# Two token-mixing layers on one core: the first block of h turned between two halves of the B combination, the folded kernel rounded by output, and the last LoRA products put among the last output's products

## The chip, the cores and the metric

The kernel runs on one core of a Trainium2 chip, as one launch. The metric is the device time of that core in microseconds (us), lower is better. Every matrix product is made from numbers split in two parts, a rounded high part and the rest, so each product of the reference costs three matmuls (high by high, low by high, high by low).

## The reference, cut to what matters

Two layers follow each other on 64 items of 32 tokens, 512 features wide. Layer 0 multiplies each item by one of 8 matrices (chosen by the item's id), then adds a plain linear layer with a gated LoRA; layer 1 is a gated MLP with per-item adapters and then a linear layer with a LoRA whose rank each token picks.

```python
# layer 0
h = einsum('bsi,boi->bso', x, weight[adapter_ids])            # "cond": one of 8 matrices per item
base_out = h @ kernel + bias
A_eff = einsum('bn,nri->bri', gate, lora_A)                    # 8 groups, 16 LoRAs of rank 32
B_eff = einsum('bn,nor->bor', gate, lora_B)
x = x + base_out + B_eff @ (A_eff @ h) + B_shared @ (A_shared @ h)
# layer 1
g, u = x W_gate + lora, x W_up + lora                          # adapters by item
h = silu(g) * u ; h = h W_down + lora
out = h W + b
scores = h @ gate_w.T + gate_b ; probs = softmax(scores)       # 4 ranks, one is picked
x = x + out + (rank-masked) h A B
```

## The kernel before, in words

The code is written by hand, engine by engine (one function each for sync, gpsimd, scalar, vector and tensor), and the order of each engine's instructions is the order of the lines; semaphores are the only link between engines. Names ending in `_hi` and `_lo` are the two parts of a number: ScalarE (ACT) makes the high part by a rounding copy (`high`, L644), VectorE (DVE) the low part as the difference (`low`, L868). Tokens are cut in NTB = 4 blocks of TB = 512.

The stages, with the time at which they run in the profile of before:

- **Sorted blocks**, up to 84.7 us. The items are sorted by their matrix into NBLK = 22 blocks of 128 rows, and the result h goes by indirect DMA (GpSimd, L573) to a scratch area in HBM in the items' own order. ACT and DVE empty the PSUM banks in turn (`evacuate`).
- **Gated A and B.** `la` (lora_a) and `gsel` (the gates spread over a diagonal) are split while the last sorted blocks run. TensorE (PE) then makes A_eff in psG and psU (48 matmuls of 256 columns), and B_eff in two halves j = 0, 1 in banks 0 and 1 of psD (12 matmuls of 512 columns each, four blocks' worth in all). ACT copies the even block of each half to `b_eff` (L714), DVE the odd one (L1119). ACT also splits `kraw`, the plain kernel with the shared LoRA folded in, in one instruction over 2048 columns.
- **First layer**, four blocks. `turn_h0(t)` turns a block of h by 16 transposes (L1475) from `tok` in SBUF into four PSUM banks psX, psT, psG, psU; `tok` is loaded from the scratch by `load_h0` on the sync queue (L513) once all scatters have landed. `high_h0` and `low_h0` split the four banks one after another into `ht`. Then come the A products into psX (L1501, L1502), `kern(o)` for the four outputs o (12 matmuls each into psD) and `lora(o)` (L1371, L1372), and DVE adds the result into x_all.
- **Gated MLP**, four blocks of 11 hidden chunks (166 to 628 us), untouched by the change.
- **Second layer**, four blocks (631 us to the end). `linear(o)` makes output o in bank o of psD (12 matmuls). `routed(t+1)` makes the next block's rank scores in psX. `turn_scores` (the four transposes of L1663) sends the scores to DVE, which runs a chain of small instructions (softmax, the pick, L1308 to L1330) to a mask `mexp`; `turn_mask` (L1671) transposes that into psU, DVE multiplies it in (`r`, L1339), ACT and DVE split `r`, and the LoRA products of the four outputs (L1366, L1367) end the block. DVE adds each output into x_all (L1345) and the sync queue stores it (L561).

Two waits of PE stand for what the change touches:

```python
                    elif o == 0:
                        pe.wait_ge(S["beff_even"], NTB // 2)
                        pe.wait_ge(S["beff_odd"], NTB // 2)
                        pe.wait_ge(S["kern_lo"], 1)
```

Of the kernel before, what the change touches and what calls it, by code (L numbers as in the profile page):

```python
# [128 lines left out]
def two_layers(nc, a, out):  # L129
    with ExitStack() as ctx:  # L130
# [179 lines left out]
        gsel_at = wh_at + slot_bytes  # L310
# [331 lines left out]
        def _(act):  # L642
# [44 lines left out]
            for b in range(NBLK):  # L687
                if b % 2 == 0:
                    evacuate(b)
                if b + AHEAD < NBLK:  # L690
                    high_xs(b + AHEAD)
                if b % W_EVERY == 0 and b // W_EVERY + 2 < N_COND:
                    high_w(b // W_EVERY + 2)
                if b == NBLK - AHEAD:
                    act.wait_ge(S["lora_a_in"], 16)
                    multiplied(act, 16)
                    high(la_hi[:], lora_a[:], S["la_hi_s"])
            act.wait_ge(S["gsel_f"], 1)
            high(g_hi[:], gsel[:], S["g_hi_s"])
# [11 lines left out]
            high(k_hi[:], kraw[:], S["kern_hi"])  # L711
            for j in range(NTB // 2):
                act.wait_ge(S["beff_ps"], j + 1)
                act.activation(b_eff[:, 2 * j, :], psD[0:R2, j, :], ACT.Copy).then_inc(S["beff_even"], 1)  # L714
            act.wait_ge(S["beff_even"], 1)
# [4 lines left out]

            high_be(0)
# [144 lines left out]
        def _(dve):  # L866
# [220 lines left out]
            for b in range(NBLK):  # L1087
# [10 lines left out]
                if b == NBLK - AHEAD:  # L1098
                    dve.wait_ge(S["gate_in"], 16)
                    dve.tensor_tensor(gsel[:].rearrange("p k (g r) -> p (k g) r", r=RANK0),  # L1100
                                      cst("delta").unsqueeze(1).broadcast_to([P, 4 * GROUPS, RANK0]),
                                      gate_v[:].rearrange("p k g -> p (k g)").unsqueeze(2)
                                      .broadcast_to([P, 4 * GROUPS, RANK0]), ALU.mult).then_inc(S["gsel_f"], 1)
                    dve.wait_ge(S["la_hi_s"], 1)
                    low(la_lo[:], lora_a[:], la_hi[:], S["la_lo_s"])
                if b == NBLK - AHEAD + 1:
                    dve.wait_ge(S["g_hi_s"], 1)
                    low(g_lo[:], gsel[:], g_hi[:], S["g_lo_s"])
# [6 lines left out]
            dve.wait_ge(S["kern_hi"], 1)  # L1115
            low(k_lo[:], kraw[:], k_hi[:], S["kern_lo"])
            for j in range(NTB // 2):
# [8 lines left out]

            low_h0(0)

# [225 lines left out]
        def _(pe):  # L1354
# [104 lines left out]
            for j in range(NTB // 2):  # L1459
# [3 lines left out]
                mm.then_inc(S["beff_ps"], 1)  # L1463
            pe.wait_ge(S["aeff_done"], 2)
# [13 lines left out]
            turn_h0(0)  # L1478

            def first_layer(t):  # L1480
                hi, lo = HT0[t % 2]

                def kern(o):
                    if t:
                        pe.wait_ge(S["x1_f"], C * (t - 1) + o + 1)
                    elif o == 0:
                        pe.wait_ge(S["beff_even"], NTB // 2)
                        pe.wait_ge(S["beff_odd"], NTB // 2)
                        pe.wait_ge(S["kern_lo"], 1)
# [159 lines left out]
            def second_layer(t):  # L1649
                hi, lo = HT2[t % 2]  # L1650

                def linear(o):
                    if t:
                        pe.wait_ge(S["out_v"], C * (t - 1) + o + 1)
                    for c in range(C):
# [4 lines left out]
                linear(0)  # L1660
                pe.wait_ge(S["r_sb"], 2 * t + 1)
                for s in range(SUB):
                    mm = pe.transpose(psG[:, s * NR:(s + 1) * NR], scores[RMAX:RS, s * P:(s + 1) * P],  # L1663
                                      ident[RMAX:RS, RMAX:RS])
                mm.then_inc(S["sc_ps"], 1)
                linear(1)
                linear(2)
                pe.wait_ge(S["mexp_s"], NR * (t + 1))
                pe.wait_ge(S["xa_m"], 2 * t)
                for s in range(SUB):  # L1670
                    pe.transpose(psU[0:RMAX, s * P:(s + 1) * P], mexp[:, s, :], ident).then_inc(S["mask_ps"], 1)  # L1671
                linear(3).then_inc(S["lin_ps"], 1)
                if t < NTB - 1:
                    routed(t + 1)
                pe.wait_ge(S["xa_hi"], t + 1)
                pe.wait_ge(S["xa_lo"], t + 1)
                for o in range(C):
# [71 lines left out]
```

## Time and profile before

| | us |
|---|---|
| median of 3 runs | 707.62 |
| lowest, highest | 703.88, 852.61 |
| the profiled execution, device time | 704.56 |
| its span, first to last instruction | 702.3 |
| PE busy in the span | 673.9 (96%) |
| DVE, ACT, POOL busy | 313.7, 294.0, 338.9 |
| mean granted TensorE clock | 0.995 |

The device time is 2.3 us more than the span. The profile shows one core; busy time of PE is modelled, so that matmuls in a row overlap slightly in the rows and their spacing, not their duration, is what one costs.

### The profile page before, as it was taken

To read this page: it belongs to the slowest core of one execution; us is meant where nothing else is said; L and a number is where in the kernel's file an instruction comes from. 1 tells how busy PE (TensorE), PEld (TensorE's weight loads), DVE (VectorE), ACT (ScalarE), POOL (GpSimd) and SP (SyncE) were. 2 spreads that over 40 slices of the span, in tenths; PEclk is the share of its full clock that TensorE was granted. 3 is DMA by queue.
4 is the path that set the end of the run, shared out by engine and by line. 5 is a ranking of instruction groups with operands and counts; after the bars stand their busy time and mean duration, and the time that the engine had idled before them with its cause. 6 is when DMAs were issued, how large, how long until landed. Compare 5 with 4: busy or idle time off the path is not lost.

```text
span 702.3 us, 11052 instructions
## 1 busy us (share of the span) xinstructions
PE 673.9 (96%) x3340; PEld 560.6 (80%) x3340; DVE 313.7 (45%) x723; ACT 294.0 (42%) x626; POOL 338.9 (48%) x262
## 2 busy tenths in 40 slices
PE   5799989998999999999999999999999999989997
PEld 3678778887788888888888888888888888867775
DVE  3778667645512222732222462242273134234664
ACT  2775553323633332653333464343265343334210
POOL 0134400231687666388666578776638867400000
PEclk9999999998999999999999999999999999999999
DMA  8963461121354346245335245434425524200112
GB/s 315 381 252 138 179 225 61 44 70 46 97 164 134 109 137 232 82 152 161 114 115 175 58 142 167 128 112 135 153 77 159 155 92 139 86 1 1 61 67 113
DMA packets 32209, 91.79 MB, mean 131 GB/s; under 512 B 5312, under 2 KB 5440, under 8 KB 30624
## 3 DMA queue, kind: packets, MB, share of 16 engines
q1 hardware_dynamic: 21936, 61.05, 25.9%
q0 software_dynamic: 10080, 30.16, 13.1%
q8 instruction: 21, 0.34, 0.2%
q14 instruction: 28, 0.23, 0.1%
q10 hardware_dynamic: 144, 0.00, 0.0%
HBM read 81.23 MB, written 9.96 MB: 130 GB/s over the span
## 4 chain that ended last, share of the span: by engine, by line
PE 86%; DVE 5%; ACT 3%; issue 2%; DMA 2%; DVEq 1%; ACTq 0%; POOL 0%; SPq 0%
PE psD L1360 10%; PE psD L1361 9%; PE psD L1362 9%; PE psG L1360 6%; PE psG L1362 6%; PE psG L1361 6%; PE psU L1360 6%; PE psU L1362 6%; PE psU L1361 6%; PE psD L1435 2%; PE psD L1436 2%; PE psD L1437 2%; PE psG L1367 1%; PE psG L1366 1%; PE psX L1360 1%
## 5 line engine op out<-in xcount | busy, mean ns | idle before, releaser
L568 POOL TENSOR_TENSOR gu_lo<-gu_raw,gu_hi 128x1024 fp32r<-128x1024 f32 x44 | 113.0, 2568 | 104.6 <-ACT gu_hi L644 104.3
L1245 DVE TENSOR_TENSOR act_f<-psU,silu 128x512 f32<-128x512 f32 x44 | 30.4, 692 | 186.1 <-ACT silu L810 186.1
L599 POOL DMA_INDIRECT ab<-in_ab,idx_tab x88 | 85.5, 972 | 20.8 <-issue 17.4
L810 ACT ACTIVATE silu<-psG 128x512 f32<-128x512 f32 x44 | 26.2, 596 | 151.3 <-PE psG L1367 151.2
L1360 PE MATMUL psG<-x_hi,gu_hi 128*128 128x512 f32 x176 | 72.6, 413 | 1.2 <-ACT silu L810 1.2
L1360 PE MATMUL psD<-act_hi,dn_hi 128*128 128x512 f32 x176 | 69.1, 393 | 0.0
L1361 PE MATMUL psD<-act_lo,dn_hi 128*128 128x512 f32 x176 | 69.1, 392 | 0.0
L1362 PE MATMUL psG<-x_hi,gu_lo 128*128 128x512 f32 x176 | 69.0, 392 | 0.0
L1360 PE MATMUL psU<-x_hi,gu_hi 128*128 128x512 f32 x176 | 68.9, 392 | 0.0
L1361 PE MATMUL psG<-x_lo,gu_hi 128*128 128x512 f32 x176 | 68.8, 391 | 0.0
L1362 PE MATMUL psD<-act_hi,dn_lo 128*128 128x512 f32 x176 | 68.7, 390 | 0.0
L1362 PE MATMUL psU<-x_hi,gu_lo 128*128 128x512 f32 x176 | 68.6, 390 | 0.0
L1361 PE MATMUL psU<-x_lo,gu_hi 128*128 128x512 f32 x176 | 68.5, 389 | 0.0
L568 POOL TENSOR_TENSOR dn_lo<-dn_raw,dn_hi 128x512 fp32r<-128x512 f32 x44 | 57.2, 1301 | 22.6 <-ACT dn_hi L644 22.6
L573 POOL DMA_INDIRECT h_scratch<-h,idx_s x22 | 23.7, 1075 | 63.2 <-ACT h L673 31.6
L602 POOL DMA_INDIRECT ad_raw<-in_ab,idx_down x44 | 45.0, 1022 | 13.4 <-issue 13.4
L644 ACT ACTIVATE gu_hi<-gu_raw 128x1024 fp32r<-128x1024 f32 x44 | 46.2, 1051 | 11.2 <-DMA gu_raw<-in_gu 11.0
L868 DVE TENSOR_TENSOR act_lo<-act_f,act_hi 128x512 fp32r<-128x512 f32 x44 | 30.6, 696 | 30.7 <-ACT act_hi L644 30.7
L644 ACT ACTIVATE act_hi<-act_f 128x512 fp32r<-128x512 f32 x44 | 27.8, 632 | 33.3 <-DVE act_f L1245 33.3
L1360 PEld LDWEIGHTS psG<-x_hi,gu_hi 128*128 128x128 f32 x176 | 33.2, 189 | 10.7 <-issue 1.2
L868 DVE TENSOR_TENSOR ad<-psX,ad 128x128 fp32r<-128x128 f32 x44 | 12.8, 291 | 63.0 <-ACT ad L644 62.8
L1435 PE MATMUL psD<-cond_w_hi,xs_t_hi 128*128 x88 | 35.6, 404 | 4.7 <-DVE cond_w_lo L868 4.7
(324 smaller groups left out, 1594.8 us busy)
## 6 DMA issues: line engine op xcount, KB each, us to landing
gu_raw<-in_gu SPq DMA_DIRECT2D x44, 512.0 KB, 3.4
dn_raw<-in_dn SPq DMA_DIRECT2D x44, 256.0 KB, 4.3
cond_w_raw<-in_cond_w SPq DMA_DIRECT2D x8, 1024.0 KB, 6.7
x_all<-in_x_t SPq DMA_DIRECT2D x4, 1024.0 KB, 9.5
tok<-h_scratch SPq DMA_DIRECT2D x4, 1024.0 KB, 5.5
out_t<-x_all SPq DMA_DIRECT2D x16, 256.0 KB, 2.1
ab<-in_ab,idx_tab POOLq DMA_INDIRECT x88, 3.8
kraw<-in_kern SPq DMA_DIRECT2D x1, 1024.0 KB, 11.5
```

The costliest lines, as they stand in the source:

```text
L568: pool.tensor_tensor(dst, x, hi, ALU.subtract).then_inc(s, 1)
L573: pool.indirect_dma_start(h0_dram, bass.IndirectOffsetOnAxis(idx_s[:, b:b + 1], 0), h0[:, ring, :], None).then_inc(S[f"c_st{ring}"], 16)
L599: pool.indirect_dma_start(ab[:, par, g, :], None, a["ab"], bass.IndirectOffsetOnAxis(idx_tab[:, NGT * t + g, fc:fc + 1], 0)).then_inc(S[f" ...
L602: pool.indirect_dma_start(ad_raw[:, par, :], None, a_rows, bass.IndirectOffsetOnAxis(idx_down[:, t, fc:fc + 1], 0)).then_inc(S[f"ad_in{par ...
L644: act.activation(dst, x, ACT.Copy).then_inc(s, 1)
L810: act.activation(silu[:], psG[:], ACT.Silu).then_inc(S["silu_s"], 1)
L868: dve.tensor_tensor(dst, x, hi, ALU.subtract).then_inc(s, 1)
L1245: dve.tensor_tensor(act_f[:], psU[:], silu[:], ALU.mult).then_inc(S["act_f_s"], 1)
L1360: pe.matmul(ps, wh, xh, start=start, stop=False, skip_group_check=True)
L1361: pe.matmul(ps, wh, xl, start=False, stop=False, skip_group_check=True)
L1362: return pe.matmul(ps, wl, xh, start=False, stop=stop, skip_group_check=True)
L1435: pe.matmul(ps, xh, w[0], start=c == 0, stop=False)
```

## The change

It moves instructions; the arithmetic stays. In five places:

1. The gates `gsel`, with their two parts, lie in slot 3 of the matrices' area instead of slot 1. Slots 0 and 1 are where the first block's `ht` goes, slots 2 and 3 the second block's.
2. In the sorted blocks, the splitting of `lora_a` and of `gsel` is written at other block numbers.
3. PE turns the first block of h between the two halves of the B combination. ACT and DVE split it right after they have taken out the first half.
4. `kraw` is split in four instructions of 512 columns, by output o, two ahead of the first block's splitting and two behind. `kern(o)` of the first block waits for its own part only.
5. In the second layer, `turn_scores` comes before `linear(0)` for the blocks t > 0; in the last block, `turn_mask` comes before `linear(2)`, and the LoRA products of outputs 0 to 2 stand in the middle of `linear(3)`.

```diff
-        gsel_at = wh_at + slot_bytes
+        gsel_at = wh_at + 3 * slot_bytes
...
-                if b == NBLK - AHEAD:
+                if b == NBLK - 4:
                     act.wait_ge(S["lora_a_in"], 16)
                     multiplied(act, 16)
                     high(la_hi[:], lora_a[:], S["la_hi_s"])
-            act.wait_ge(S["gsel_f"], 1)
-            high(g_hi[:], gsel[:], S["g_hi_s"])
+                if b == NBLK - 2:
+                    act.wait_ge(S["gsel_f"], 1)
+                    high(g_hi[:], gsel[:], S["g_hi_s"])
...
+            high_kern(0)
+            high_kern(1)
+            take_even(0)
             high_h0(0)
+            high_kern(2)
+            high_kern(3)
+            take_even(1)
+            act.wait_ge(S["beff_even"], 1)
+            high_be(0)
...
+            low_kern(0)
+            low_kern(1)
+            take_odd(0)
             low_h0(0)
+            low_kern(2)
+            low_kern(3)
+            take_odd(1)
...
+            two_blocks_b(0)
             pe.wait_ge(S["aeff_done"], 2)
...
             turn_h0(0)
+            two_blocks_b(1)
...
+                    else:
+                        if o < NTB // 2:
+                            pe.wait_ge(S["beff_even"], o + 1)
+                            pe.wait_ge(S["beff_odd"], o + 1)
+                        pe.wait_ge(S["kern_lo"], o + 1)
...
+                if t:
+                    turn_scores()
+                    linear(0)
+                else:
+                    linear(0)
+                    turn_scores()
+                linear(1)
+                if t < NTB - 1:
+                    linear(2)
+                    turn_mask()
+                    linear(3).then_inc(S["lin_ps"], 1)
+                    routed(t + 1)
+                    lora(0)
+                    lora(1)
+                    lora(2)
+                else:
+
+                    turn_mask()
+                    linear(2)
+                    linear(3, range(2))
+                    lora(0)
+                    lora(1)
+                    lora(2)
+                    linear(3, range(2, C))
+                lora(3)
```

What this does to the engines, at three places. First PE from the last product of the first half of B to the A products of the first block, before; `lora_b` by `gsel` is a B product, `tok` a transpose of h.

```order
579 L1362 MATMUL psD<-lora_b_hi,gsel_lo 128x512
580 L1360 MATMUL psD<-lora_b_hi,gsel_hi 128x512
...
591 L1362 MATMUL psD<-lora_b_hi,gsel_lo 128x512
592 L1475 MATMUL psX<-const,tok_178 128x128 x4
593 L1475 MATMUL psT<-const,tok_178 128x128 x4
594 L1475 MATMUL psG<-const,tok_178 128x128 x4
595 L1475 MATMUL psU<-const,tok_178 128x128 x4
596 L1501 MATMUL psX<-ht_hi,ae 128x512
```

The same rows of the changed kernel:

```order
579 L1383 MATMUL psD<-lora_b_hi,gsel_lo 128x512
580 L1499 MATMUL psX<-const,tok_178 128x128 x4
581 L1499 MATMUL psT<-const,tok_178 128x128 x4
582 L1499 MATMUL psG<-const,tok_178 128x128 x4
583 L1499 MATMUL psU<-const,tok_178 128x128 x4
584 L1381 MATMUL psD<-lora_b_hi,gsel_hi 128x512
...
595 L1383 MATMUL psD<-lora_b_hi,gsel_lo 128x512
596 L1527 MATMUL psX<-ht_hi,ae 128x512
```

The 16 transposes moved ahead of twelve B products, which now stand between them and the A products. Next ACT in the same place, before:

```order
250 L644 ACTIVATE ae<-a_eff 128x4x64
251 L644 ACTIVATE kern_hi<-kraw 128x2048
252 L714 ACTIVATE b_eff<-psD 64x512 x2
253 L644 ACTIVATE be_h<-b_eff 64x512 x2
254 L644 ACTIVATE be_m<-b_eff 64x512
255 L644 ACTIVATE ht_hi<-psX 128x512
```

and in the changed kernel:

```order
250 L644 ACTIVATE ae<-a_eff 128x4x64
251 L644 ACTIVATE kern_hi<-kraw 128x4x128 x2
252 L719 ACTIVATE b_eff<-psD 64x512
253 L644 ACTIVATE ht_hi<-psX 128x512
...
256 L644 ACTIVATE ht_hi<-psU 128x512
257 L644 ACTIVATE kern_hi<-kraw 128x4x128 x2
258 L719 ACTIVATE b_eff<-psD 64x512
259 L644 ACTIVATE be_h<-b_eff 64x512 x2
260 L644 ACTIVATE be_m<-b_eff 64x512
```

The copy of the second half of B and the three instructions on `be` moved behind the splitting of h. Last, DVE in the last sorted blocks, where the splitting of A stands. Before:

```order
274 L1073 COPY h_71<-psD 128x512
275 L1100 TENSOR_TENSOR gsel<-const,gate_v 128x1024
276 L868 TENSOR_TENSOR lora_a_lo<-lora_a,lora_a_hi 128x2048
277 L868 TENSOR_TENSOR gsel_lo<-gsel,gsel_hi 128x1024
278 L1073 COPY h_71<-psD 128x512
```

and in the changed kernel:

```order
274 L1084 COPY h_71<-psD 128x512
275 L1111 TENSOR_TENSOR gsel<-const,gate_v 128x1024
276 L879 TENSOR_TENSOR lora_a_lo<-lora_a,lora_a_hi 128x2048
277 L879 TENSOR_TENSOR gsel_lo<-gsel,gsel_hi 128x1024
278 L1084 COPY h_71<-psD 128x512
```

Nothing moved there: between the old and the new block number these engines have no other instruction.

## Rows read from the trace of the kernel before

**Rows 1.** Waits of PE: who it waited for, us in total, times, longest

```profile
PE psX L1360 <- DVE hta_lo L868: 3.3, 1, 3.3
PE psX L1501 <- DVE ht_lo L868: 2.1, 1, 2.1
PE psG L1360 <- DVE gsel_lo L868: 0.8, 1, 0.8
PE psD L1366 <- DVE r_lo L868: 0.2, 1, 0.2
```

**Rows 2.** Timeline of PE, 94 to 104 us: start, us, instruction

```profile
94.10 0.39 PE L1360 MATMUL psD<-lora_b_hi,gsel_hi 128*128 128x512 f32 x1
...
96.82 0.60 PE L1475 MATMUL psX<-const,tok 128*128 128x128 f32 x4
...
98.13 0.60 PE L1475 MATMUL psU<-const,tok 128*128 128x128 f32 x4
100.80 0.47 PE L1501 MATMUL psX<-ht_hi,ae 128*128 128x512 f32 x1 [2.06 <-DVE ht_lo L868]
...
103.06 0.40 PE L1360 MATMUL psD<-ht_hi,kern_hi 128*128 128x512 f32 x1
```

**Rows 3.** Timeline of ACT, 92 to 100 us

```profile
92.51 1.90 ACT L644 ACTIVATE kern_hi<-kraw 128x2048 fp32r<-128x2048 f32 x1
...
97.02 0.59 ACT L714 ACTIVATE b_eff<-psD 64x512 f32<-64x512 f32 x1 [2.13 <-PE psD L1362]
...
99.33 0.60 ACT L644 ACTIVATE ht_hi<-psX 128x512 fp32r<-128x512 f32 x1
```

**Rows 4.** Timeline of DVE, 99 to 103 us

```profile
99.96 0.69 DVE L868 TENSOR_TENSOR ht_lo<-psX,ht_hi 128x512 fp32r<-128x512 f32 x1 [1.90 <-ACT ht_hi L644]
...
101.76 0.68 DVE L868 TENSOR_TENSOR ht_lo<-psU,ht_hi 128x512 fp32r<-128x512 f32 x1
```

**Rows 5.** Sync queue's timeline at 89 us, then first load's landing, then all four loads'

```profile
89.38 0.94 SPq L513 DMA_DIRECT2D tok<-h_scratch  x2
...
tok<-h_scratch SPq DMA_DIRECT2D x1, 1024.0 KB, 5.6
...
DMA to landing us min/median/max: 5.4/5.5/7.7
```

**Rows 6.** Timeline of PE, 117 to 120 us: the A products of the second block

```profile
117.55 0.39 PE L1501 MATMUL psX<-ht_hi,ae 128*128 128x512 f32 x1
...
119.39 0.39 PE L1360 MATMUL psD<-ht_hi,kern_hi 128*128 128x512 f32 x1
```

**Rows 7.** Timeline of PE in the last block of the second layer

```profile
684.06 0.39 PE L1360 MATMUL psD<-htb_hi,wf_hi 128*128 128x512 f32 x1
...
692.79 0.60 PE L1671 MATMUL psU<-const,mexp 128*64 128x128 f32 x4
...
695.78 0.39 PE L1362 MATMUL psD<-htb_hi,wf_lo 128*128 128x512 f32 x1
696.36 0.47 PE L1366 MATMUL psD<-r_hi,rb 128*128 128x512 f32 x1 [0.19 <-DVE r_lo L868]
```

**Rows 8.** Timeline of DVE in the last block of the second layer

```profile
687.33 0.17 DVE L1308 COPY soft<-psG 128x16 f32<-128x16 f32 x1 [1.74 <-PE psG L1663]
...
690.56 0.50 DVE L1330 COPY mexp<-soft 128x32 f32<-128x32 f32 x4
...
695.52 0.69 DVE L868 TENSOR_TENSOR r_lo<-r,r_hi 128x512 fp32r<-128x512 f32 x1 [0.70 <-ACT r_hi L644]
697.11 2.73 DVE L1345 SCALAR_TENSOR_TENSOR x_all<-psD,bias,x_all 128x512 f32<-128x512 f32 x4 [0.89 <-PE psD L1367]
```

**Rows 9.** Busy by window: us, PE, PEld, DVE, ACT, POOL (instructions), granted PE clock, DMA, GB/s

```profile
160.00:180.00 20.00, 16.73 (x75) 14.16 (x73) 13.06 (x28) 8.00 (x24) 2.43 (x2) 0.83 0.13 41
620.00:640.00 20.00, 16.72 (x86) 13.29 (x86) 9.29 (x35) 10.92 (x32) 0.00 (x0) 1.00 0.01 1
```

**Rows 10.** Timeline of PE at the first MLP block, after its last first-layer product

```profile
169.86 0.55 PE L1360 MATMUL psX<-x_hi,at_hi 128*128 128x256 f32 x1 [3.27 <-DVE x_lo L868]
```

More of the change, by code:

```diff
@@ L710, in _, with high_kern, take_even @@
             high(ae[:, :, 0:R2], ae_of(0), S["ae_s"])
-            high(k_hi[:], kraw[:], S["kern_hi"])
-            for j in range(NTB // 2):
+            def high_kern(o):
+                at = slice(o * P, o * P + P)
+                high(k_hi[:, :, at], kraw[:, :, at], S["kern_hi"])
+            def take_even(j):
                 act.wait_ge(S["beff_ps"], j + 1)
                 act.activation(b_eff[:, 2 * j, :], psD[0:R2, j, :], ACT.Copy).then_inc(S["beff_even"], 1)
-            act.wait_ge(S["beff_even"], 1)
             def high_be(t):
@@ L719, in high_be @@
                 high(be_m[R2:2 * R2], b_eff[:, t, :], S["be_s"])
-            high_be(0)
             def high_h0(t):
@@ L1103, in _ @@
                                       .broadcast_to([P, 4 * GROUPS, RANK0]), ALU.mult).then_inc(S["gsel_f"], 1)
+                if b == NBLK - AHEAD + 1:
                     dve.wait_ge(S["la_hi_s"], 1)
                     low(la_lo[:], lora_a[:], la_hi[:], S["la_lo_s"])
-                if b == NBLK - AHEAD + 1:
                     dve.wait_ge(S["g_hi_s"], 1)
@@ L1114, in _, with low_kern, take_odd @@
             low(ae[:, :, R2:2 * R2], ae_of(0), ae[:, :, 0:R2], S["ae_l"])
-            dve.wait_ge(S["kern_hi"], 1)
-            low(k_lo[:], kraw[:], k_hi[:], S["kern_lo"])
-            for j in range(NTB // 2):
+            def low_kern(o):
+                at = slice(o * P, o * P + P)
+                dve.wait_ge(S["kern_hi"], o + 1)
+                low(k_lo[:, :, at], kraw[:, :, at], k_hi[:, :, at], S["kern_lo"])
+            def take_odd(j):
                 dve.wait_ge(S["beff_ps"], j + 1)
@@ L1458, in _, with two_blocks_b @@
             pe.wait_ge(S["lb_lo_s"], 1)
-            for j in range(NTB // 2):
+            def two_blocks_b(j):
                 for k in range(4):
@@ L1485, in kern @@
                         pe.wait_ge(S["x1_f"], C * (t - 1) + o + 1)
[L1486 to L1489, printed above, removed]
+                    else:
[3 more added lines that the diff above has]
+                        pe.wait_ge(S["kern_lo"], o + 1)
                     for c in range(C):
@@ L1650, in second_layer, with linear @@
                 hi, lo = HT2[t % 2]
-                def linear(o):
+                def linear(o, part=range(C)):
                     if t:
                         pe.wait_ge(S["out_v"], C * (t - 1) + o + 1)
-                    for c in range(C):
+                    for c in part:
                         mm = product(psD[:, o, :], both(wf_hi, wf_lo, al, c, slice(o * P, o * P + P)),
@@ L1658, in linear @@
                     return mm
[L1660 to L1677, printed above, removed]
+                def turn_scores():
+                    pe.wait_ge(S["r_sb"], 2 * t + 1)
+                    for s in range(SUB):
+                        mm = pe.transpose(psG[:, s * NR:(s + 1) * NR], scores[RMAX:RS, s * P:(s + 1) * P],
+                                          ident[RMAX:RS, RMAX:RS])
+                    mm.then_inc(S["sc_ps"], 1)
@@ L1678, in second_layer, with turn_mask, lora @@
+                def turn_mask():
+                    pe.wait_ge(S["mexp_s"], NR * (t + 1))
+                    pe.wait_ge(S["xa_m"], 2 * t)
+                    for s in range(SUB):
+                        pe.transpose(psU[0:RMAX, s * P:(s + 1) * P], mexp[:, s, :], ident).then_inc(S["mask_ps"], 1)
+                def lora(o):
+                    if o == 0:
+                        pe.wait_ge(S["xa_hi"], t + 1)
+                        pe.wait_ge(S["xa_lo"], t + 1)
                     stacked(psD[:, o, :], rb[:, o * P:o * P + P], r64_hi[:], r64_lo[:], False, True
```

## The prediction

> **What bounds the kernel now.** I read the page's busy times first: PE is busy 96% of the span, so a gain can come only from the 28 us in which it is not, or from less matmul work, and this change takes no matmul away. Next I read the waits of PE [rows 1], and ask of each whether the change is near it. Three are: 0.8 us for the low part of the gates ahead of the A combination, 2.1 us for the low part of the first block of h, and 0.2 us for the low part of `r` in the last block. The 3.3 us ahead of the second layer stays, and so does its like ahead of the MLP [rows 10]. Then I followed the two places in the timelines of the engines [rows 2 to 4, 7, 8]. A last look went to the granted clock by stretch [rows 9], since an idle PE can cost more than its idle time. What is saved ahead of 104 us comes through to the end if nothing later waits for something other than PE. The chain of waits speaks for that: it is mostly PE, and at the later joints it goes through ACT and DVE work that itself began behind a PE product.
>
> **The splitting of A (point 2 of the change): nothing.** On ACT and DVE the instructions stand in the same order as before, as the lists ahead show, since neither engine has anything between the old block number and the new one. The waits are the same as well. The 0.8 us for `gsel_lo` [rows 1] stay. The moved slot of the gates is only room for point 3.
>
> **The first block of h (point 3).** Before, PE made the second half of B from 94.10, turned h from 96.82 to 98.57 (98.13 and 0.44 for the last four transposes), and stood till 100.80 [rows 2]. ACT could not take the first bank before 99.33, as it had the second half of B at 97.02 and `be` till 99.3 in front of it [rows 3]; DVE followed at 99.96 [rows 4]. So the stall is the latency of the split plus 1.8 us of other ACT work. DVE also set the pace of the four A products: they took 103.06 - 100.80 = 2.26 us, where the second block's took 119.39 - 117.55 = 1.84 us [rows 6].
>
> In the changed kernel PE is free for the turn at 94.10. Is h there? The load was issued at 89.38 and took 5.6 us to land [rows 5], which is 94.98. In before nobody saw that, for the second half of B covered it. The cover is gone, so PE waits 0.9 us. The sum from there:
> - turn: 94.98 + 1.75 = 96.73
> - second half of B: 96.82 - 94.10 = 2.72 us, so 99.45
> - split of h beside it: the first bank is full 0.6 us after the turn begins, at 95.6, and ACT is free then, as the copy of the first half of B, due at 94.3, is short (0.59, rows 3). From ACT's start at 99.33 to DVE's last end (101.76 + 0.68) it took 3.1 us [rows 3, 4], so the split is done at 98.7, 0.7 us ahead of PE
> - A products without a wait: 99.45 + 1.84 = 101.29, against 103.06.
>
> The gain is **1.8 us**. It would be 103.06 - (94.10 + 1.75 + 2.72 + 1.84) = 2.65 if h were there in time, and the new wait takes 0.9 of it. The last B half and `be` now come behind the split on ACT; they are needed for `lora(0)`, two outputs (24 products, 5.4 us) after the A products, at 106.7. ACT starts on them at 99.7 and needs about 0.6 + 1.8 us, so they are ready by 102.2.
>
> **The plain kernel in four parts (point 4): nothing by itself.** `kern_hi` is 1.90 us for 2048 columns [rows 3], so about 0.5 to 0.6 each. Two parts on ACT fit between 92.5 and 94.3, where the whole instruction stood before, and two behind the split, under PE's B half and A products. Each adds an instruction's overhead of some 0.1 us on engines with slack there. If the pieces were not made, ACT would still be ready; the bound is 0 to 0.1 us.
>
> **The tail (point 5).** In the last block PE runs without a gap from 684.06 on; its last product before the LoRA starts at 695.78, the next could follow 0.23 later, at 696.01, and starts at 696.36 [rows 7]. So PE waits 0.35 us for `r_lo`, of which the profile, which models the ends, shows 0.2. What ends last is not PE, though, but DVE: its four additions start at 697.11 and take 2.73, one after another at 0.68, to 699.84 [rows 8]. The span ends 2.46 later, with the store.
>
> Now PE's last LoRA pair stands alone at the end. The PE work from 684.06 is the same 11.95 us, plus three LoRA pairs at twice 0.23, 1.4 us, so the last pair starts at 697.4. An addition starts 0.75 us after its pair's start (696.36 to 697.11), so at 698.1, and ends at 698.8. The three other additions are over by then: their pairs start near 694.6, 695.1 and 695.6. That is 699.84 - 698.8 = **1.1 us** less.
>
> It needs `r` in time. The scores are turned 2.7 us earlier; DVE is at the previous block's additions till 1.74 us before it takes the scores at 687.33 (its idle time in that row), so the soft chain starts at 685.6, and ends 1.7 us earlier, near 689.3 [rows 8]. `turn_mask` moves ahead of `linear(2)`, to 692.79 - 2.75 = 690.0 [rows 7]: the mask is there, with 0.7 us to spare. `r_lo` ended 3.4 us after `turn_mask` began (692.79 to 696.21, rows 7, 8), so 693.5. PE comes to `lora(0)` at 694.6. In the blocks t = 1 and 2 the earlier `turn_scores` waits for ACT's copy of the scores, which is over by the time the previous LoRA products are; PE has no gap there now and gets none, gain 0.
>
> **Sum.** 1.8 + 1.1 = 2.9 us: span 702.3 - 2.9 = 699.4, device time 704.56 - 2.9 = **701.7 us**. The 704.56 of the profiled run lies between the 703.88 and 707.62 of the runs shown; 852.61 stands by itself. The difference of the two, 3.7 us, is larger than what the change brings, and that leads to the clock.
>
> **The clock.** Rows 9 show the granted clock at 0.83 over 160 to 180 us, so at 1.2 GHz for 0.17 x 20 / 0.5 = 6.8 us of it; PE had stood 3.27 us ahead of the MLP [rows 10]. Over 620 to 640 it stays at 2.4 GHz, though PE stood 3.28 us there too [rows 1, 9]. Two idle times alike, one with a drop and one without: it is a matter of when, not of how long. Half speed over 6.8 us costs 3.4 at most; part of it fell into the idle time, so I take 3.0 for the one in before.
>
> The Trainium skill, "TensorE: Matmul & The Clock Gate", "What's actually happening", says that the monitor behind the clock runs free of the kernel, so that the same kernel sees its transitions at different places. The two rows agree, and by that rule a shift of 1.8 us may turn either of them, in any run.
>
> **Rivals.**
> - *A second drop*, ahead of the second layer. The 3.3 us idle there [rows 1] is as long as the one that fell. Everything up to 640 us lies 1.8 us earlier and may meet the clock otherwise. Price: 6.8 us at half speed, up to 3.4. 701.7 + 3.4 = 705.1, slower than before. It decides from 2.9 us on, that is when PE works in 5.8 of the 6.8 us. For it: equal idle times. Against: nothing in before fell there.
> - *No drop*: the same in the other direction, 701.7 - 3.0 = 698.7.
> - *h lands late.* The four loads took 5.4 to 7.7 us [rows 5]; at 7.7 the turn starts at 97.1, and B and the A products end at 103.4: point 3 loses 0.3 us, the tail's 1.1 stays, and the time is 703.8. Against: the load of the first block is the first in its queue, and its issue does not move.
> - *h lands early*, before 94.10: the gain is 2.65 and the time 700.8. Nothing in the rows says so. The Trainium skill, "DMA: Bandwidth & Descriptors", "Anatomy of one DMA", gives some 2.0 us plus the bytes at 436 GB/s, 4.4 us for this 1 MB, an estimate by which h would be there at 93.8. The row says 5.6, and the sum goes by the row.
> - *The tail doesn't hide*: the mask is late, PE waits before `linear(2)` by more than 0.7 us, and the tail's gain goes. 701.7 + 1.1 = 702.8.
>
> **How the numbers follow.** Forecast (one drop, as in before) 0.50; second drop 0.17; no drop 0.12; h late 0.08; h early 0.05; tail 0.05; something else 0.03. The range takes in no drop and the second drop, 698.7 to 705.1, and holds the rest between them; what is left out is mostly unknown offsets of a session. All cases lie within 14 us of 707.62, the 2% that a measurement of this kernel can tell from no change, so faster by that and slower by that get 0.01 each.
>
> **What would show it.** In the changed profile: PE stands about 0.9 us ahead of the first transposes near 95.0, and not at all ahead of the A products, which start near 99.5; `ht_hi` on ACT starts near 95.6; the wait for `gsel_lo` is still 0.8; the waits for `r_lo` are gone, DVE's last addition starts 0.7 us after the last LoRA pair and is alone. A transposing wait of 2 us, or an A product that still waits for `ht_lo`, would refute point 3; an idle PE ahead of the mask's transposes, point 5. A clock row below 1 near 627 would say that the clock, not the order, made the time.

## The result and the profile after

The changed kernel took 701.87 us (median; 700.74 to 703.96), the kernel before 706.46 us on the same chip. Two of its 17 runs, 844.83 and 852.61 us, were in a slow state and stand outside the ratio. That ratio is 0.9942 with an interval of 0.9929 to 0.9955, so 3.2 to 5.0 us less, 4.1 in the middle. The forecast was 701.7 us. The profiled execution took 701.42 us with a span of 699.4, which is 2.9 us less span than before. So the two profiled runs differ by what the sum said, and the ratio by 1.2 us more (0.3 to 2.1 by its interval); the experiments are mostly about that rest.

The waits of PE, after (who it waited for, us in total, times, longest), beside [rows 1]:

```profile
PE psX L1381 <- DVE hta_lo L879: 3.3, 1, 3.3
...
PE psX L1499 <- issue: 0.5, 1, 0.5
PE psG L1381 <- DVE gsel_lo L879: 0.3, 1, 0.3
```

The waits for `ht_lo` (2.1) and `r_lo` (0.2) are gone, and a wait ahead of the transposes of h has come in. The timeline of PE there, beside [rows 2]:

```profile
93.32 0.39 PE L1383 MATMUL psD<-lora_b_hi,gsel_lo 128*128 128x512 f32 x1
94.22 0.63 PE L1499 MATMUL psX<-const,tok 128*128 128x128 f32 x4 [0.52 <-issue]
...
95.92 0.48 PE L1381 MATMUL psD<-lora_b_hi,gsel_hi 128*128 128x512 f32 x1
...
98.75 0.39 PE L1527 MATMUL psX<-ht_hi,ae 128*128 128x512 f32 x1
...
100.60 0.39 PE L1381 MATMUL psD<-ht_hi,kern_hi 128*128 128x512 f32 x1
```

The transposes begin at 94.22; the next product could have followed the last of B's first half at 93.32 + 0.23 = 93.55, so 0.67 us are lost. The sync queue shows for what:

```profile
88.65 1.12 SPq L513 DMA_DIRECT2D tok<-h_scratch  x2
```

The load's issue at 88.65 and PE's start at 94.22 lie 5.6 us apart, the landing time of [rows 5]. The profile names no releaser for this wait (`issue`); that it is the landing is tested below, with three products of B in front of the turn. Then B's second half runs, and the A products follow 0.23 us behind its last product and 0.23 us apart: 98.75 to 100.60 is 1.85 us. The split of h had run beside B, as the timelines of ACT and DVE show:

```profile
94.89 0.60 ACT L644 ACTIVATE ht_hi<-psX 128x512 fp32r<-128x512 f32 x1 [0.56 <-PE psX L1499]
...
98.95 0.59 ACT L719 ACTIVATE b_eff<-psD 64x512 f32<-64x512 f32 x1 [0.96 <-PE psD L1383]
```

```profile
95.52 0.69 DVE L879 TENSOR_TENSOR ht_lo<-psX,ht_hi 128x512 fp32r<-128x512 f32 x1 [0.90 <-ACT ht_hi L644]
...
97.32 0.68 DVE L879 TENSOR_TENSOR ht_lo<-psU,ht_hi 128x512 fp32r<-128x512 f32 x1
```

`ht_lo` is done at 98.0, before PE asks for it at 98.75, and the copy of B's second half is now behind the split on ACT instead of in front of it [rows 3].

The last block, PE beside [rows 7] and DVE beside [rows 8]:

```profile
688.15 0.60 PE L1697 MATMUL psU<-const,mexp 128*64 128x128 f32 x4
...
692.72 0.40 PE L1387 MATMUL psD<-r_hi,rb 128*128 128x512 f32 x1
...
695.51 0.39 PE L1387 MATMUL psD<-r_hi,rb 128*128 128x512 f32 x1
695.74 0.40 PE L1388 MATMUL psD<-r_lo,rb 128*128 128x512 f32 x1
```

```profile
683.58 0.16 DVE L1329 COPY soft<-psG 128x16 f32<-128x16 f32 x1
...
686.81 0.50 DVE L1351 COPY mexp<-soft 128x32 f32<-128x32 f32 x4
...
690.88 0.69 DVE L879 TENSOR_TENSOR r_lo<-r,r_hi 128x512 fp32r<-128x512 f32 x1 [0.70 <-ACT r_hi L644]
693.39 2.07 DVE L1366 SCALAR_TENSOR_TENSOR x_all<-psD,bias,x_all 128x512 f32<-128x512 f32 x3 [1.82 <-PE psD L1388]
696.18 0.75 DVE L1366 SCALAR_TENSOR_TENSOR x_all<-psD,bias,x_all 128x512 f32<-128x512 f32 x1 [0.72 <-PE psD L1388]
```

Three additions run under the last products and one stands alone, 0.67 us behind the last pair's start. It ends at 696.93, and the span 2.5 us later.

The clock by window (columns as in [rows 9]):

```profile
160.00:180.00 20.00, 15.81 (x78) 13.23 (x77) 11.94 (x27) 8.61 (x24) 5.22 (x3) 0.91 0.12 41
620.00:640.00 20.00, 16.72 (x76) 12.72 (x76) 9.65 (x43) 10.28 (x30) 0.00 (x0) 0.91 0.01 1
```

0.91 over 20 us is 1.2 GHz for 0.09 x 20 / 0.5 = 3.6 us. In place of one low stretch of 6.8 us [rows 9] there are two of about half that length, one at each of the 3.3-us idle times.

Between fixed points of the two profiled runs the time went so:

| from | before | after | difference |
|---|---|---|---|
| start to the first A combination | 85.50 | 84.95 | -0.55 |
| to the first product of the plain kernel | 17.56 | 15.65 | -1.91 |
| to the last product of the first layer | 63.14 | 63.12 | -0.02 |
| to the first MLP product | 3.66 | 3.66 | 0.00 |
| MLP's first 24 products (clock) | 5.26 | 4.43 | -0.83 |
| to the LoRA products ahead of the last block (clock) | 507.08 | 508.47 | +1.39 |
| to the end of DVE's last addition | 17.64 | 16.65 | -0.99 |
| to the end of the span | 2.46 | 2.47 | 0.01 |

The two rows with the clock (together 0.56 us dearer than before) and the first row (0.55 us cheaper) cancel to 0.0, which is luck. The first row is no work of the change: the first A combination began between 84.6 and 86.3 us in the thirteen profiles, in kernels of either order, and the wait for `gsel_lo`, 0.3 instead of 0.8 here, was 0.2 to 0.8 in the runs of either order below. What is left is the order.

### The profile page after: what moved, and what is told of

Same layout as the page of the kernel before. It is cut to its first block, busy times and chain, and to the rows that moved or that the text cites. A ratio compares the mean times of both kernels' runs of the same rounds, so it can differ in the third digit from the quotient of the medians.

```text
span 699.4 us, 11059 instructions
## 1 busy us (share of the span) xinstructions
PE 673.2 (96%) x3340; PEld 560.0 (80%) x3340; DVE 314.1 (45%) x726; ACT 295.4 (42%) x629; POOL 339.7 (49%) x262
## 4 chain that ended last, share of the span: by engine, by line
PE 89%; DVE 3%; ACT 2%; DMA 2%; issue 2%; DVEq 1%; ACTq 0%; POOL 0%; SPq 0%
PE psD L1381 10%; PE psD L1382 10%; PE psD L1383 10%; PE psG L1381 6%; PE psG L1383 6%; PE psG L1382 6%; PE psU L1381 6%; PE psU L1383 6%; PE psU L1382 6%; PE psD L1456 2%; PE psD L1458 1%; PE psD L1457 1%; PE psG L1388 1%; PE psG L1387 1%; PE psT L1388 1%
## 5 line engine op out<-in xcount | busy, mean ns | idle before, releaser
L599 POOL DMA_INDIRECT ab<-in_ab,idx_tab x88 | 86.3, 981 | 20.7 <-issue 16.9
L644 ACT ACTIVATE bu<-ab 128x512 fp32r<-128x512 f32 x44 | 27.4, 623 | 30.2 <-DMA ab<-in_ab,idx_tab 30.1
```

The source lines that it names most:

```text
L599: pool.indirect_dma_start(ab[:, par, g, :], None, a["ab"], bass.IndirectOffsetOnAxis(idx_tab[:, NGT * t + g, fc:fc + 1], 0)).then_inc(S[f" ...
L644: act.activation(dst, x, ACT.Copy).then_inc(s, 1)
```

## The experiments

All ratios are to the kernel before, run on the same chip in turn. Unless it says otherwise the whole kernel is computed.

**Points 1 to 4 alone.** The changed kernel with the second layer's order of before:

```diff
+                linear(0)
+                pe.wait_ge(S["r_sb"], 2 * t + 1)
...
+                linear(1)
+                linear(2)
+                pe.wait_ge(S["mexp_s"], NR * (t + 1))
...
+                linear(3).then_inc(S["lin_ps"], 1)
+                if t < NTB - 1:
+                    routed(t + 1)
...
-                if t:
-                    turn_scores()
-                    linear(0)
-                else:
-                    linear(0)
-                    turn_scores()
-                linear(1)
...
-                    turn_mask()
-                    linear(2)
-                    linear(3, range(2))
...
-                    linear(3, range(2, C))
-                lora(3)
```

> The changed kernel with the second layer's PE order put back, so points 1 to 4 alone. Theory (each point works in its place by itself): the profile has the wait ahead of the first transposes (0.5 to 0.9 us) and none ahead of the A products; the stretch from the first A combination product to the first plain product is 15.65 us as in the changed kernel, against 17.56 before; the tail is as before (last addition of DVE in a row of four, wait for r_lo). Gain 1.9 us, about 0.997 of before. Rival (the two points share a gain, as when the clock makes it): 1 us or less, or 3 us.

Median 703.17 against 705.15, ratio 0.9968 [0.9952, 0.9984]: 1.1 to 3.4 us less. Its waits of PE:

```profile
PE psG L1381 <- DVE gsel_lo L879: 0.8, 1, 0.8
PE psX L1499 <- issue: 0.7, 1, 0.7
...
PE psD L1387 <- DVE r_lo L879: 0.2, 1, 0.2
```

The tail's wait for `r_lo` is back, the one for `ht_lo` is not. So the turn in the middle of B makes the gain of its stage by itself: 15.85 us from the A combination to the plain kernel, against 17.56 before and 15.65 in the changed kernel, where the wait for h was 0.5 instead of 0.7. The end of the kernel takes 17.63 us from the LoRA products ahead of the last block, as before.

**Point 5 alone.** The kernel before with the second layer of the changed one, the same lines with the signs turned.

> The kernel before with point 5 alone. Theory: from the last block's start to the end 1.1 us less than before, last addition alone, the wait ahead of the A products still 2.1 us; 0.9985 of before. Rival (the store of the last output, not DVE, sets the end): no gain in the span although DVE ends earlier.

Median 704.21, ratio 0.9986 [0.9969, 1.0002]. The middle, 1.0 us, is what was worked out, though the interval just takes in no gain. The profile is sharper: the end takes 16.65 us, as in the changed kernel, against 17.64 before. In its waits of PE `r_lo` is missing and `ht_lo` stands at 2.1. The two parts add up to 2.0 + 0.9 = 2.9 us in medians. This profile had something that the profile of before did not show, here the windows around the first block of h and two spans of PE's timeline in them:

```profile
100.00:104.00 4.00, 2.84 (x9) 1.59 (x10) 2.48 (x4) 1.75 (x4) 0.00 (x0) 0.81 0.88 261
104.00:108.00 4.00, 4.00 (x15) 3.25 (x14) 3.45 (x8) 1.46 (x3) 0.00 (x0) 0.77 0.00 1
```

```profile
101.16 0.47 PE L1501 MATMUL psX<-ht_hi,ae 128*128 128x512 f32 x1 [2.06 <-DVE ht_lo L868]
...
103.56 0.63 PE L1502 MATMUL psX<-ht_lo,ae 128*64 128x512 f32 x1
103.99 0.63 PE L1360 MATMUL psD<-ht_hi,kern_hi 128*128 128x512 f32 x1
```

PE had turned h for 1.7 us and stood for 2.1, and from about 102.3 to 105.7 its products are 0.43 us apart instead of 0.23: the clock was at 1.2 GHz for (0.19 + 0.23) x 4 / 0.5 = 3.4 us. The order of before thus has a third place where the clock can fall, and it is the one that point 3 takes away. The next runs test whether this makes the rest of the gain.

**The two late idle times filled.** 13 products of 512 columns into a free bank, whose result nobody reads, go into each of the two 3.3-us idle times (behind the first layer and behind the MLP), in the changed kernel and in the kernel before. The same extra products, with this purpose alone, stand in all further kernels called "filled".

```diff
+            def fill(w, x):
+                for k in range(13):
+                    pe.matmul(psT[:], w, x[k % len(x)], start=True, stop=True, skip_group_check=True)
+            fill(ht1_hi[:, 0, 0:P], [ht1_hi[:, c, :] for c in range(C)])
...
+            fill(td_hi[:, 0:P], [td_hi[:]])
```

> The changed kernel, with 13 matmuls of 512 columns added in each of the two 3.3 us idle times of PE (ahead of the MLP and ahead of the second layer); they write a PSUM bank that nothing reads and change no result. Clock theory: with PE at work there the granted clock is 1.00 over 160 to 180 and 620 to 640 us, where the changed kernel has 0.91 and 0.91; 24 products of 256 columns take 2.9 us and 12 of 512 columns 2.8 us; 3.1 us less than the 699.4 of its profile, and less spread between runs. Rival: the added work delays the products behind it as much as the clock gives back, or the clock falls all the same: no gain, or a loss of up to 1 us.

> The kernel before with the same 26 added matmuls. Clock theory: 702.3 less 2.9 us. The measured ratio of after to before (0.9942, 4.1 us) is 1.2 us more than the 2.9 of the two profiles; if the clock drops make that difference, this kernel and the filled changed kernel differ by the 2.9 us of the order alone (699.3 against 696.3 of span) and their ratio is 0.9957. Rival (the 1.2 us come from the order, at a place that the profiled run did not show): the two filled kernels differ by 4 us.

The changed kernel filled took 699.48, ratio 0.9924 [0.9900, 0.9947]; the kernel before filled 703.66, ratio 0.9977 [0.9961, 0.9993]. With the late windows at full clock in both, they are still 4.2 us apart in medians, as far as the two kernels of the case. So the filled pair, with the late places out of play, still shows more than the 2.9 us of the order. (That does not say that the late places add nothing in the two kernels of the case, where they do fall.) The windows of the two, the changed kernel first:

```profile
100.00:104.00 4.00, 4.00 (x20) 3.22 (x19) 2.92 (x7) 2.67 (x6) 0.00 (x0) 1.00 0.32 119
...
160.00:180.00 20.00, 18.76 (x97) 15.33 (x96) 12.62 (x28) 9.57 (x26) 6.43 (x4) 1.00 0.19 54
620.00:640.00 20.00, 19.69 (x98) 15.45 (x97) 11.79 (x46) 9.86 (x30) 0.00 (x0) 1.00 0.01 1
```

```profile
100.00:104.00 4.00, 3.05 (x9) 1.84 (x10) 2.48 (x4) 1.54 (x4) 0.00 (x0) 0.72 0.85 260
104.00:108.00 4.00, 4.00 (x17) 3.20 (x16) 3.52 (x8) 1.46 (x3) 0.00 (x0) 0.85 0.00 0
```

The fall near 102 us is there again in the kernel before. Of its 12 runs one has a mean clock of 1.0, and a span of 699.6; the eleven others have 0.996 or 0.998, and spans of 700.6 to 702.4. Only the profiled one shows where the clock fell; that it was the same place in the ten others is inferred from the mean clocks.

**The third place filled too.** The kernel before, with the 26 products and eight more in the 2.1 us ahead of the first A product:

```diff
             turn_h0(0)
+            for k in range(8):
+                pe.matmul(psD[:, 3, :], lb_hi[:, k % 4, 0:P], lb_hi[:, k % 4, :], start=True, stop=True,
+                          skip_group_check=True)
```

> The kernel before with the 26 added matmuls of the last experiment and 8 more in the 2.1 us idle time ahead of the A products (into a PSUM bank that the first plain products open anew; no result changes). In the profile of before with the two late places filled, the clock was low from about 102 to 106 us, right behind the 16 transposes and that idle time, and 11 of its 12 runs had a mean clock below 1. Theory (the rest of the measured gain is the clock at that third place, which the change also takes away): clock 1.00 throughout, 1.5 to 2 us less than with two places filled, 701.9 us median or less, and 3 us more than the filled changed kernel. Rival (that place falls by the transposes, whatever stands behind them): still low near 102 us in most runs, 703.7.

Median 702.28, ratio 0.9952 [0.9936, 0.9969]. PE still waits 0.2 us for `ht_lo`, and the plain kernel begins 17.57 us after the A combination, as in before (17.56), so the eight products brought nothing but the clock:

```profile
100.00:104.00 4.00, 3.77 (x16) 2.34 (x16) 3.18 (x6) 1.41 (x3) 0.00 (x0) 1.00 0.68 246
```

In medians it is 1.4 us faster than with the late places filled alone (1.8 by the two ratios). These are two sessions on two chips; the table below gives the same price from single profiles. And it is 2.8 us slower than the changed kernel filled (2.0 by the ratios, each uncertain by 1.2 to 1.7 us; 3.0 by the spans of the profiles): with the clock at 2.4 GHz at all three places in both profiles, that is what the order brings.

**The third place filled alone.** The kernel before with the eight products only.

> The kernel before with only the 8 added matmuls ahead of the A products. Clock theory: the clock is not low near 102 us in any run, so the runs with a mean clock of 0.99 to 0.993 (13 of 29, 7 of 11 of the kernel before) become few, and the median falls by 1.2 us (0.998). Rival (the clock at that place fell only in the kernel with the other places filled): mean clocks and median as before.

Median 705.00 against 705.89, ratio 0.9989 [0.9976, 1.0001]. The windows of its profile:

```profile
100.00:104.00 4.00, 3.77 (x16) 2.17 (x15) 3.18 (x6) 1.41 (x4) 0.00 (x0) 1.00 0.71 247
...
160.00:180.00 20.00, 16.44 (x77) 13.77 (x76) 13.06 (x29) 8.85 (x27) 3.56 (x2) 0.91 0.12 41
620.00:640.00 20.00, 16.72 (x78) 12.75 (x77) 8.44 (x34) 10.33 (x31) 0.00 (x0) 0.91 0.01 1
```

The interval just takes in no gain, so these runs support the account of the third place and do not settle it. The mean clocks of the single runs say more: 11 of its 12 runs have 0.994 or 0.995, and one has 0.990. Of the 18 runs of before beside them 10 have 0.994 or 0.995, and eight have 0.992 or 0.990.

**The same stages in eight profiles.** The times between fixed instructions, in us:

| kernel | A combination to plain kernel | to the first layer's last product | first MLP product to the LoRA products ahead of the last block | to DVE's last addition |
|---|---|---|---|---|
| before | 17.56 | 63.14 | 512.34 | 17.64 |
| points 1 to 4 alone | 15.85 | 63.12 | 512.93 | 17.63 |
| point 5 alone | 18.13 | 64.02 | 512.29 | 16.65 |
| before, late places filled | 18.28 | 63.76 | 510.06 | 17.63 |
| before, all places filled | 17.57 | 63.14 | 509.97 | 17.64 |
| before, third place filled | 17.58 | 63.14 | 512.79 | 17.64 |
| changed | 15.65 | 63.12 | 512.90 | 16.65 |
| changed, late places filled | 15.50 | 63.12 | 510.03 | 16.66 |

The last column has the tail's gain of 1.0 us wherever point 5 is in, and nowhere else. The first two columns give the price of the third place directly: 1.45 us in the kernel with point 5 alone and 1.34 in the one with the late places filled, more than before. The third column gives the price of the late places: 2.3 to 2.4 us for the one stretch of 6.8, 2.9 for the two of 3.4.

**The scores turned late.** The changed kernel, with `turn_scores` behind `linear(0)` in every block:

```diff
-                if t:
-                    turn_scores()
-                    linear(0)
-                else:
-                    linear(0)
-                    turn_scores()
+                linear(0)
+                turn_scores()
```

> The changed kernel with the scores' transposes behind linear(0) again, as before; the mask's transposes stay ahead of linear(2) in the last block. Theory (the tail needs the earlier scores): the soft chain starts 1.7 us later, the mask is ready 1.0 us after PE comes to its transposes, PE waits 1.0 to 1.1 us there, nothing takes it back, and the tail's gain of 1.1 us is gone. Rival (the chain has enough room either way): no wait, the end as in the changed kernel.

One run, 703.74 us. A wait of PE and three rows of DVE:

```profile
PE psU L1697 <- DVE mexp L1351: 0.9, 1, 0.9
```

```profile
686.64 0.17 DVE L1329 COPY soft<-psG 128x16 f32<-128x16 f32 x1 [1.74 <-PE psG L1689]
...
689.87 0.50 DVE L1351 COPY mexp<-soft 128x32 f32<-128x32 f32 x4
...
698.48 0.75 DVE L1366 SCALAR_TENSOR_TENSOR x_all<-psD,bias,x_all 128x512 f32<-128x512 f32 x1 [0.72 <-PE psD L1388]
```

DVE is again idle for 1.74 us ahead of the softmax, and PE stands 0.9 us ahead of the mask's transposes. From the LoRA products ahead of the last block to the last addition it takes 17.72 us, so the whole gain of the tail is gone (17.64 before, 16.65 changed). Moving the mask and the LoRA products pays only together with the earlier scores. (Of this run's longer span another 0.9 us is a start-up wait for `cond_w_lo`, 5.6 instead of 4.7, which has nothing to do with the edit.)

**The split of the plain kernel alone.** The kernel before with `kern_hi` and `kern_lo` made in four parts, in the old place:

```diff
-            high(k_hi[:], kraw[:], S["kern_hi"])
+            for o in range(C):
+                at = slice(o * P, o * P + P)
+                high(k_hi[:, :, at], kraw[:, :, at], S["kern_hi"])
```

> The kernel before with the plain kernel split in four instructions on ACT and on DVE, all four in the old place. Theory: four times 0.6 in a row with 0.5 us spacing on ACT, some 2.0 us for all against 1.90, 0.1 us later for the first b_eff copy, nothing on PE: wait of 2.1 us ahead of the A products, within 0.2. Rival (the strided pieces are slow): more than 0.8 us each, the wait grows.

One run, 704.36 us, a span of 701.8. ACT and PE:

```profile
92.02 2.18 ACT L644 ACTIVATE kern_hi<-kraw 128x512 fp32r<-128x512 f32 x4
```

```profile
PE psX L1506 <- DVE ht_lo L870: 2.1, 1, 2.1
```

The four parts take 0.28 us more than the one instruction [rows 3], the wait for `ht_lo` stays at 2.1, and the plain kernel begins 17.56 us after the A combination, as before. By itself point 4 moves nothing; it makes room for the split of h between its halves.

**Three products of B in front of the turn.** The changed kernel filled, with the first three of the twelve products of B's second half moved ahead of the transposes, under the wait for h:

```diff
             two_blocks_b(0)
+            two_blocks_b(1, range(1))
             pe.wait_ge(S["aeff_done"], 2)
...
             turn_h0(0)
-            two_blocks_b(1)
+            two_blocks_b(1, range(1, 4))
```

> The filled changed kernel, with the first 3 of the 12 products of the second half of B put ahead of the transposes. Theory (the wait ahead of the transposes is the landing of the load of h, 5.6 us from its issue, and can be covered): the wait of 0.5 to 0.9 us is gone or below 0.1, the stretch from the first A combination product to the first plain product is 15.1 instead of 15.65 us, and no wait comes ahead of the A products, whose first input is ready 1.9 us early; 0.5 us less. Rival (the wait is a switch of TensorE into transposing, not a landing): it stays at 0.5, no gain.

Median 698.37, ratio 0.9895 [0.9879, 0.9911], 1.1 us less than without the edit (699.48), but in another session and on another chip. Its profile is the better witness, here PE's timeline:

```profile
94.65 0.39 PE L1383 MATMUL psD<-lora_b_hi,gsel_lo 128*128 128x512 f32 x1
94.89 0.63 PE L1501 MATMUL psX<-const,tok 128*128 128x128 f32 x4
...
100.59 0.39 PE L1381 MATMUL psD<-ht_hi,kern_hi 128*128 128x512 f32 x1
```

No wait ahead of the transposes, and 15.00 us from the A combination to the plain kernel instead of 15.50. So the wait was the landing of h and not a cost of turning to transposes, and the 0.5 us can be had back.

**The gates earlier.** The changed kernel with DVE's product for the gates two sorted blocks sooner:

```diff
-                if b == NBLK - AHEAD:
+                if b == NBLK - 5:
                     dve.wait_ge(S["gate_in"], 16)
```

> The changed kernel with DVE's product that spreads the gates two sorted blocks earlier (behind block 17's copy instead of block 19's), so that the splitting of A's operands really ends earlier. Theory (behind the gates the landing of h is next, and it hangs on the scatters): the wait for gsel_lo of 0.3 to 0.8 us goes, the A and B combinations start that much earlier, the wait ahead of the transposes grows by the same (to 1.0 to 1.3 us), the transposes start no earlier, no gain. Rival (each wait counts): 0.3 to 0.8 us less, the wait ahead of the transposes stays at 0.5 to 0.7.

Median 701.36, ratio 0.9946 [0.9929, 0.9964]: no gain over the changed kernel. PE and DVE:

```profile
PE psG L1381 <- DVE gsel_lo L879: 0.3, 1, 0.3
```

```profile
81.14 2.29 DVE L879 TENSOR_TENSOR lora_a_lo<-lora_a,lora_a_hi 128x2048 fp32r<-128x2048 f32 x1 [0.81 <-ACT lora_a_hi L644]
83.35 1.22 DVE L879 TENSOR_TENSOR gsel_lo<-gsel,gsel_hi 128x1024 fp32r<-128x1024 f32 x1
```

This was a miss: the wait did not go. DVE now stands 0.81 us for ACT's `lora_a_hi`, and `gsel_lo`, next in its queue, comes hardly sooner. What DVE waits for is ACT's step, and the experiment did not touch it.

**Everything together.** The filled kernel with six of B's twelve products in front of the turn, and the earlier gates.

> The filled changed kernel, gates two blocks earlier and 6 of the 12 products of the second half of B ahead of the transposes. Theory (with enough products to cover the landing the earlier gates do count): no wait for gsel_lo, at most 0.1 us ahead of the transposes, none ahead of the A products; 0.5 us less than the version with 3 products ahead (698.4), so 697.9. Rival: the transposes now come late enough for the split of h to be late, and PE waits ahead of the A products.

Median 697.83, ratio 0.9893 [0.9872, 0.9913], with PE's waits at `gsel_lo` 0.2 and none ahead of the transposes or the A products; its stage takes 14.96 us. It cannot be told from the kernel with three products in front, and the wait for `gsel_lo` was expected to go and did not quite. Both beat the two kernels of this case: in medians by 3.5 and 4.0 us the changed one (another session), by 7.4 and 8.1 us the one before.

## Why the prediction was right, point by point

**The A split and the gates' slot: nothing.** Right. The wait for `gsel_lo`, predicted to stay at 0.8, was 0.3 in the profile after and 0.8 in the run of points 1 to 4 alone. It lies between 0.2 and 0.8 in the runs of either order, so it is a matter of the run.

**The first block of h: 1.8 us.** It was 1.91. The terms: the pace of the unwaited A products was right (1.84 foreseen, 1.85 measured). The turn took 1.70 us for 1.75, the second half of B 2.83 for 2.72. The new wait was 0.67 us from slot to slot against 0.9, since B's first half ended 4.90 us behind the load's issue (88.65 to 93.55) instead of 4.72 [rows 2, 5]; the landing was 5.6 as foreseen. ACT and DVE had the split done 0.75 us ahead of PE, 0.7 foreseen. The rival by which h is there before B's first half ends did not come: 5.6 us from issue to PE's start. The Trainium skill's formula ("DMA: Bandwidth & Descriptors", "Anatomy of one DMA") gives an estimate of 4.4 us for it, but the section states it for DMAs issued by GpSimd, and this load is issued by the sync engine; here the measured time decides.

**The plain kernel in four: 0 to 0.1 us.** Nothing on PE; on ACT 0.28 us, hidden.

**The tail: 1.1 us.** It was 0.99. The mask had 0.84 us to spare (`mexp` ends at 687.3, the transposes come at 688.15), 0.7 foreseen, and `r_lo` 1.15 us (691.57 to 692.72), 1.1 foreseen. The run with the scores turned late shows that this rests on the earlier `turn_scores`, and the table that the 1.0 us comes with point 5 and goes with it.

**The sum: 2.9 us.** The order brought 1.91 + 0.99 = 2.9, the spans of the profiled runs differ by 2.9, and the two filled kernels with the clock full at all three places differ by 2.8 in medians, though these are of two sessions and chips. That the forecast of 701.7 us lies 0.2 from the measured median is luck. It was taken from one execution of before, 704.56 us, which was 1.9 below the median of 706.46, and the gain came out 1.2 us larger; the two nearly cancel. The ratio that the forecast implies, 0.9959, lies just outside the measured interval of 0.9929 to 0.9955.

**The clock.** The forecast took one low stretch of 6.8 us, as before, in the likeliest case. What came in the profiled run was two of about 3.4, one at each late place, and they cost 2.9 us by the table, where the one of before had cost 2.3 to 2.4 (the forecast put it at 3.0). The sign that the prediction names for the clock did come, a row below 1 near 627 (0.91 over 620 to 640); it stands for a loss of 1.4 us there, so it did not make the gain. The rivals with a second long drop or none did not come as stated, though single runs show a part of both: mean clocks of 0.998 in five, 0.995 in nine and 0.993 in three of the 17 runs, with mean spans of 699.1, 699.7 and 701.6. The Trainium skill ("TensorE: Matmul & The Clock Gate", "What's actually happening") has the monitor running free of the kernel. The spread over runs of one kernel agrees. The profiles are more regular than that: the three kernels in which PE stands 2.1 us ahead of the A products and nothing is filled (before, point 5 alone, the plain kernel split alone) all show one stretch of 6.8 us behind the first layer and none behind the MLP, and the five others without filled late places (changed, points 1 to 4, late scores, early gates, third place filled) all show 0.91 at both. No experiment was made on this.

**What the forecast missed** is 1.2 us of the 4.1. It looked for the clock only at the two 3.3-us idle times, because the profiled run of before has 1.00 at 102 us. Other executions of the old order have not (0.81 with point 5 alone, 0.72 with the late places filled). An estimate from mean clocks: 3.4 us at half speed is 0.0024 of a span of 700, so 0.998, 0.995, 0.993 and 0.990 stand for one to four such stretches. The 29 runs of before in the first session (16 at 0.995 or 0.994, nine at 0.993 or 0.992, four at 0.990) had 2.6 on average, the 17 of the changed kernel 1.9. The 0.7 that are missing, at 1.2 to 1.6 us each (from the mean spans: 699.1 to 701.6 over two steps after, 702.1 to 705.3 over two before; the single steps are unequal, 0.6 to 2.0), are 0.9 to 1.1 us. So the clock can account for the rest. How much of it is the third place is less clear:

- With the late places filled it accounts for all: it fell in 11 of 12 runs (by their mean clocks) at 1.3 to 1.45 us each, and 2.9 and 1.3 make the 4.2 us by which the filled pair differs.
- Without them it can have fallen in fewer runs. Of the 58 runs of before in the three sessions half (29) have a mean clock of 0.993 or less, and filling the third place alone was worth 0.9 us (with an interval that just takes in nothing).
- The late places may give the remainder. Five of 17 runs of the changed kernel have 0.998, and none of the 58 of before.

That the clock falls at the third place before the change, and costs 1.3 to 1.45 us where it does, is shown. That the third place makes most of the 1.2 is only likely, and the 1.2 itself lies near the size of its interval. Which idle time falls in which run, and why 3.4 us in one and 6.8 in another, stays open.

## What to carry to other kernels

A stall of the bounding engine is often the latency of a short chain through two other engines; put work that is ready into it, and check what the moved step now waits for itself, here a load that the old order had covered. Work at the very end pays by what must follow it: leave only one product and one addition behind the last wait, and move the start of the side chain by as much. Read the clock from several runs and not from one profile: an idle time that cost nothing extra in the profiled run cost 1.3 to 1.45 us in others, and a few useless products in idle times gave back 0.9 us (one place) to 2.4 us (two places, the changed kernel's 701.87 to 699.48, in different sessions). Compare a forecast with the measured ratio too: a time taken from one run of before can hit by luck.

## What was not expected of the hardware

- The clock fell behind 1.7 us of transposes and 2.1 us of idle PE, to 1.2 GHz for 3.4 us (products of 512 columns 0.43 us apart instead of 0.23). No idle time there was over 2.1 us. With eight products in the idle time, and the transposes as they were, it stayed at 1.00.
- Low stretches were of two lengths, about 3.4 and 6.8 us, and equal idle times of 3.3 us led to none and a long one in the profile of before, and to two short ones in that of the changed kernel.
- Products whose results nobody reads, in the idle times alone, kept the granted clock at 1.00 in those windows of all profiles that had them.
- Start-up waits that no edit touched moved by up to 1.2 us between runs (`onehot` 7.9 to 9.1, `cond_w_lo` 4.7 or 5.6), which is as much as the tail brings. One run can't tell such an edit by its time; its waits can.
